# Ranks of a top-2 expert routing: doubling sums replaced by segmented scans, slots computed earlier on VectorE

## The reference, cut to what matters

```python
scores = sigmoid(x @ router_w)                    # 4096 x 16
_, top_idx = top_k(scores + expert_bias, 2)       # ties: the lower index wins
gates = sum(one_hot(top_idx) * top_scores)
shared_out = (silu(x @ w1) * (x @ w2)) @ w3       # all tokens
for e in range(16):                               # routed
    acc += (silu(xf @ w1[e]) * (xf @ w2[e])) @ w3[e] * gates[:, e]
out = x + tanh(g_ffn) * (shared_out + acc)
```

## Time and profile before

| | us |
|---|---|
| median of the runs (3) | 642.24 |
| lowest, highest | 637.35, 643.82 |
| span of the profiled execution | 568.1 |
| median less that span | 74.1 |
| PE busy in the span | 538.4 (95%) |
| DVE busy | 399.6 (70%) |
| ACT busy | 307.6 (54%) |
| POOL busy | 270.1 (48%) |

### The profile page before, as it was taken

One profiled execution on the slowest core, in us unless ns is written; L12 is line 12 of the kernel. 1 busy time (PEld: TensorE's weight loads), 2 busy tenths in 40 slices (PEclk: granted clock), 3 DMA queues, 4 the chain that ended last, 5 costly groups with the idle time before them and its releaser, 6 DMA issues.

```text
span 568.1 us, 13109 instructions
## 1 busy us (share of the span) xinstructions
PE 538.4 (95%) x4164; PEld 348.7 (61%) x4164; DVE 399.6 (70%) x890; ACT 307.6 (54%) x594; POOL 270.1 (48%) x257
## 2 busy tenths in 40 slices
PE   4899799999989999994999999999999999999997
PEld 2467676756556656653566666666666655665664
DVE  1432888867797867772788888888888736677675
ACT  2324666785226665651677777777777733333332
POOL 3001475453417787876443444334443035666770
PEclk9659999999999999997999999999999999999999
DMA  8999626338504120011233333333334123374442
GB/s 223 313 351 310 224 104 222 115 110 284 180 1 152 55 74 20 2 37 35 81 103 105 112 104 109 103 100 113 110 105 107 57 56 104 93 250 121 140 135 88
DMA packets 53228, 72.55 MB, mean 128 GB/s; under 512 B 8032, under 2 KB 43424, under 8 KB 53168
## 3 DMA queue, kind: packets, MB, share of 16 engines
q1 hardware_dynamic: 43984, 51.75, 27.9%
q0 software_dynamic: 8608, 17.91, 11.7%
q10 hardware_dynamic: 576, 2.10, 1.1%
HBM read 49.64 MB, written 22.09 MB: 126 GB/s over the span
## 4 chain that ended last, share of the span: by engine, by line
PE 68%; POOL 14%; DVE 6%; issue 5%; DMA 4%; SPq 1%; ACT 1%; DVEq 0%; POOLq 0%; ACTq 0%
PE bank L1568 17%; PE bank L1472 17%; POOL slot_token L550 12%; PE bank L1493 8%; PE bank L1594 8%; PE bank L1578 4%; PE bank L1308 3%; PE bank L1552 3%; DMA WR<-in_ctx_t 2%; PE bank L1335 2%; PE bank L1297 1%; POOL X L518 1%; DVE STAGE L917 1%; DMA xrow<-STAGE 1%; PE bank L1382 1%
## 5 line engine op out<-in xcount | busy, mean ns | idle before, releaser
L1472 PE MATMUL bank<-XTC,WS 128*128 128x512 f16 x768 | 176.1, 379 | 0.5 <-DVE ROWS L1213 0.5
L1472 PEld LDWEIGHTS bank<-XTC,WS 128*128 128x128 f16 x768 | 74.8, 98 | 78.9 <-issue 1.0
L567 POOL DMA_INDIRECT ROWS<-xrow,idx x72 | 76.8, 1067 | 97.0 <-PE bank L1552 83.7
L1568 PE MATMUL bank<-WR,XTB 128*64 x432 | 100.4, 382 | 0.7 <-DVE STAGE L1219 0.7
L1568 PE MATMUL bank<-STAGE,XTB 128*64 128x512 f16 x432 | 100.4, 382 | 0.0
L584 POOL DMA_INDIRECT ROWS<-yrow,posi x64 | 63.8, 997 | 55.0 <-DMA yrow<-ROWS 26.8
L550 POOL DMA_INDIRECT slot_token<-tokid,sloti x64 | 72.2, 1129 | 34.9 <-issue 19.2
L798 ACT ACTIVATE STAGE<-WR 128x1024 f16 x72 | 76.7, 1066 | 18.2 <-PE bank L1594 17.9
L720 ACT ACTIVATE SIL<-bank 128x512 f32<-128x512 f32 x63 | 37.6, 597 | 81.1 <-PE bank L1472 79.9
L1568 PEld LDWEIGHTS bank<-WR,XTB 128*64 128x64 f16 x432 | 44.7, 110 | 44.1 <-issue 7.7
L1112 DVE SCALAR_TENSOR_TENSOR G<-bank,SIL 128x512 f32<-128x512 f32 x63 | 43.4, 690 | 29.7 <-ACT SIL L720 29.0
(11 more groups left out here) (171 smaller groups left out, 874.5 us busy)
## 6 DMA issues: line engine op xcount, KB each, us to landing
WR<-in_routed_w SPq DMA_DIRECT2D x39, 256.0 KB, 5.3
yrow<-ROWS SPq DMA_DIRECT2D x72, 128.0 KB, 1.7
X<-in_x SPq DMA_DIRECT2D x4, 1024.0 KB, 13.0
xrow<-STAGE SPq DMA_DIRECT2D x8, 512.0 KB, 2.9
xtd<-STAGE SPq DMA_DIRECT2D x8, 512.0 KB, 2.6
out<-X SPq DMA_DIRECT2D x7, 512.0 KB, 3.3
WR<-in_ctx_t SPq DMA_DIRECT2D x4, 768.0 KB, 10.8
WR<-in_shared_w SPq DMA_DIRECT2D x3, 1024.0 KB, 14.4
```

The source lines that it names most:

```text
L567: pool.indirect_dma_start(out=XG[:, u, :], out_offset=None, in_=xrow, in_offset=bass.IndirectOffsetOnAxis(ap=idx[:, b:b + 1].bitcast(U32), ...
L1472: last = pe.matmul(acc[:, :], WS[:, wx, at:at + P], XTC[:, u, xx, k, :], start=(k == 0 and m == 0), stop=(k == KD - 1 and m == 2))
L1568: last = pe.matmul(bank[u][part, :], XTB[:, b % 4, xx, k, part], w[s], start=(k == 0 and m == 0), stop=(k == KD - 1 and m == 2), tile_posi ...
```

## The change

- `choose_lowest` now runs one segmented scan (`tensor_tensor_scan`, state = state * NEXT + EQ, where `NEXT_E` is 0 at the first expert of a tile and 1 elsewhere) and one `scalar_tensor_tensor` in place of a multiplication, a reduction and a comparison. `rev` and its iota are gone.
- `OHS`, the rank tables and the totals lie expert by tile (`[E, NT]`) where they lay tile by expert; `OHS` is written, and `PA` read, through a transposed view.
- `take_totals` and the five `sum_tiles` become one scan that reads bank 7. `before` is now minus the other triangle with the diagonal, so that the subtraction of the totals (L1052) goes. `sum_experts` has 5 instructions where it had 10, a scan of 16 elements among them, and counts rows, not blocks.
- The order on DVE: `sum_experts` and `slots_of_all` come ahead of `gate_hidden(8)`; both `slots_of_choice` and `table_slots` ahead of `gate_hidden(9)`; then `add_shared(0)` and `block_experts`. `gates` comes ahead of `gate_hidden(12)`.
- POOL takes the low half of step 9 also (POOL_TO from J + 1 to J + 2, J = 8), ahead of its scatters.
- `prepare` fills two tables of 512 elements and clears their first columns, where it cleared two of 256 and two of 8.

```diff
-        POOL_FROM, POOL_TO = 2, J + 1
+        POOL_FROM, POOL_TO = 2, J + 2
...
-            pool.memset(before[:, :], 1.0).then_inc(c_mem, 1)
+            pool.memset(before[:, :], -1.0).then_inc(c_mem, 1)
...
-                link(dve.tensor_tensor(RE, EQ, over_tiles(rev[:, :]), ALU.mult))
-                link(dve.tensor_reduce(rm[:, :], RE, AX.X, ALU.max))
-                link(dve.tensor_tensor(OH[k], over_experts(rm[:, :]), over_tiles(rev[:, :]), ALU.is_equal))
+                link(dve.tensor_tensor_scan(out=rows_flat(RE), data0=rows_flat(NEXT_E), data1=rows_flat(EQ),
+                                            initial=0.0, op0=ALU.mult, op1=ALU.add))
+                link(dve.scalar_tensor_tensor(out=OH[k], in0=RE, scalar=1.0, in1=EQ,
+                                              op0=ALU.is_equal, op1=ALU.mult))
...
-            def take_totals():
+            def sum_tiles():
+
                 dve.wait_ge(rank, 2)
-                link(dve.tensor_copy(rows_flat(INCA[:, PADT:PADT + NT, :]), bank[7][:, :]))
...
+                link(dve.tensor_tensor_scan(out=rows_flat(INC), data0=rows_flat(NEXT_T), data1=bank[7][:, :],
+                                            initial=0.0, op0=ALU.mult, op1=ALU.add))
+
+            def sum_experts():
+
+                link(dve.tensor_scalar(ni[:, :], INC[:, :, NT - 1], float(PR - 1), None, ALU.add))
                 link(dve.tensor_scalar(bi[:, :], ni[:, :], PR.bit_length() - 1, None, ALU.arith_shift_right))
...
+                link(dve.tensor_scalar(bf[:, :], bi[:, :], float(PR), None, ALU.mult))
+                link(dve.tensor_tensor_scan(out=ea[:, :], data0=ones[:, 0:E], data1=bf[:, :],
+                                            initial=0.0, op0=ALU.mult, op1=ALU.add))
+                link(dve.tensor_tensor(base_row[:, :], ea[:, :], bf[:, :], ALU.subtract))
+
+            def slots_of_all():
+
+                link(dve.tensor_tensor(PB, INC, base_row[:, :].unsqueeze(2).to_broadcast([P, E, NT]), ALU.add))
                 link(dve.tensor_tensor(rows_flat(PA), rows_flat(PB), bank[6][:, :], ALU.add))
 
             def slots_of_choice(k):
-                link(dve.tensor_tensor(EQ, OH[k], PA, ALU.mult))
+                link(dve.tensor_tensor(EQ, OH[k], PA.rearrange("p e t -> p t e"), ALU.mult))
...
-            dve.tensor_tensor(OHS, OH[0], OH[1], ALU.add).then_inc(ohs_ready, 1)
+            dve.tensor_tensor(OHS.rearrange("p e t -> p t e"), OH[0], OH[1], ALU.add).then_inc(ohs_ready, 1)
             gate_hidden(7, 1, pool=4)
-            take_totals()
-            sum_tiles(INCA, INCB, 1)
-            sum_tiles(INCB, INCA, 2)
-            sum_tiles(INCA, INCB, 4)
+            sum_tiles()
+            sum_experts()
+            slots_of_all()
             gate_hidden(8, 0, pool=5)
-            sum_tiles(INCB, INCA, 8)
-            sum_tiles(INCA, INCB, 16)
-            ends = sum_experts(INCB)
-            gate_hidden(9, 1, pool=6)
-            hidden_lo(9, 1)
-            add_shared(0)
-            gate_hidden(10, 0, pool=7)
-            slots_of_all(INCB)
-            hidden_lo(10, 0)
-            block_experts(ends)
-            gate_hidden(11, 1)
             slots_of_choice(0)
-            hidden_lo(11, 1)
             slots_of_choice(1)
             table_slots()
+            gate_hidden(9, 1, pool=6)
+            add_shared(0)
+            block_experts()
+            gate_hidden(10, 0, pool=7)
+            hidden_lo(10, 0)
+            gate_hidden(11, 1, pool=8)
+            hidden_lo(11, 1)
+            gates()
             gate_hidden(12, 0)
-            gates()
             hidden_lo(12, 0)
```

More of the change, by code:

```diff
@@ L181, in flamingo_block @@
         OH1 = arena([NT, E])
-        OHS = arena([NT, E])
-        INCA = arena([NT // 2 + NT, E])
-        INCB = arena([NT // 2 + NT, E])
-        PA = arena([NT, E])
-        PB = arena([NT, E])
+        OHS = arena([E, NT])
+        INC = arena([E, NT])
+        PA = arena([E, NT])
+        PB = arena([E, NT])
+        NEXT_E = arena([NT, E])
+        NEXT_T = arena([E, NT])
         UNDER = -(-arena_at[0] // SLOT)
@@ L207, in flamingo_block @@
         bf = sb("bf", [P, E], F32)
[L208 to L209 removed]
+        ea = sb("ea", [P, E], F32)
         base_row = sb("base_row", [P, E], F32)
@@ L491, in _ @@
             pool.affine_select(out=before[:, :], in_=before[:, :], compare_op=ALU.is_ge, fill=0.0,
-                               base=-1, pattern=[[1, P]], channel_multiplier=-1).then_inc(c_ready, 1)
-            pool.iota(row_iota[:, :], pattern=[[1, PARTS]], base=0, channel_multiplier=PARTS,
+                               base=0, pattern=[[-1, P]], channel_multiplier=1).then_inc(c_ready, 1)
+            pool.iota(row_iota[:, :], pattern=[[PR, PARTS]], base=0, channel_multiplier=PARTS * PR,
                       allow_small_or_imprecise_dtypes=True)
@@ L500, in _ @@
                                    base=2 - k, pattern=[[-4, NW]], channel_multiplier=1).then_inc(c_mem, 1)
-            pool.iota(rev[:, :], pattern=[[-1, E]], base=E, channel_multiplier=0,
-                      allow_small_or_imprecise_dtypes=True).then_inc(c_ready, 1)
             pool.memset(SDROW, 0.0).then_inc(sdrow_zero, 1)
@@ L1021, in gates @@
                     link(dve.tensor_scalar(gate[:, k, :], gsum[:, :], tgs[:, :], None, ALU.mult))
-            def take_totals():
+            def sum_tiles():
                 dve.wait_ge(rank, 2)
-                link(dve.tensor_copy(rows_flat(INCA[:, PADT:PADT + NT, :]), bank[7][:, :]))
-            def sum_tiles(src, dst, step):
-                link(dve.tensor_tensor(dst[:, PADT:PADT + NT, :], src[:, PADT:PADT + NT, :],
-                                       src[:, PADT - step:PADT - step + NT, :], ALU.add))
@@ L1032, in sum_experts @@
-            def sum_experts(inc):
-                link(dve.tensor_scalar(ni[:, :], inc[:, PADT + NT - 1, :], float(PR - 1), None, ALU.add))
-                link(dve.tensor_scalar(bi[:, :], ni[:, :], PR.bit_length() - 1, None, ALU.arith_shift_right))
-                dve.tensor_copy(bf[:, :], bi[:, :])
-                link(dve.tensor_copy(ea[:, PADE:PADE + E], bi[:, :]))
-                es, ed = ea, eb
-                step = 1
-                while step < E:
-                    link(dve.tensor_tensor(ed[:, PADE:PADE + E], es[:, PADE:PADE + E],
-                                           es[:, PADE - step:PADE - step + E], ALU.add))
-                    es, ed = ed, es
-                    step *= 2
-                ends = es[:, PADE:PADE + E]
-                link(dve.tensor_tensor(nf[:, :], ends, bf[:, :], ALU.subtract))
-                link(dve.tensor_scalar(base_row[:, :], nf[:, :], float(PR), None, ALU.mult))
-                return ends
@@ L1067, in table_slots, with block_experts @@
                                          in1=highi[:, :, :], op0=ALU.mult, op1=ALU.add).then_inc(slots_ok, 1)
-            def block_experts(ends):
+            def block_experts():
                 for s in range(PARTS):
-                    last = dve.tensor_scalar(ended[:, s, :], ends, row_iota[:, s:s + 1], None, ALU.is_le)
+                    last = dve.tensor_scalar(ended[:, s, :], ea[:, :], row_iota[:, s:s + 1], None, ALU.is_le)
                 link(last)
```

19 lines of the change are left out of this document (4 added, 15 removed).

## The result

| | us |
|---|---|
| median of the kernel after (4 runs) | 656.51 (655.24 to 658.9) |
| median of the kernel before beside it (4 runs) | 643.03 (637.35 to 650.64) |
| ratio after / before | 1.0215, 95% interval 1.0161 to 1.0269 |
| profiled execution of after: own time, span | 658.9, 656.8 |

What follows compares the result with a forecast made beforehand. PE was taken as the bound, with one wait for rows behind POOL's scatters. Gains of 7.95 (wait), 0.8 (`add_shared(0)`) and 2.4 (clock), 11.15 us, took 642.24 to 631.1 us; 8-in-10 range 627 to 637.5.

Steps and rivals of the forecast that it cites:

- The step that failed: Whole kernel: terms counted from the profile's 568.1 us span, the 74.1 us up to the 642.24 median left unchanged.
- the 7.95 us: PE's wait at the first `block_transpose` for fetched rows: gone entirely, rows ready 1.6 us ahead of PE.
- I take nothing: Seven scatter issues moved from 248-258 to 158-168 us: worth between -2 and +4.6 us, counted as nothing.
- Rival 3: DVE's scans run as a slow recurrence: whole gain eaten from 5.7 us a scan, 649 at 8 us; chance 0.03.
- The dense instruction of `choose_lowest`: DVE's choices: one dense instruction of 0.68 us beside the scan, making each choice 0.7 us shorter.
- From bank 7 to `sloti`'s end: DVE's stretch from reading bank 7 to the finished slots: 12.9 us earlier, at 155.3 against 168.23.
- `add_shared(0)`: DVE's step ahead of PE's `late_rows(8)`: runs earlier, gaining 0.8 of PE's 1.63 us wait.
- Scatters: POOL's 64 scatters: first starts at about 158.2, 10.3 us earlier; count and pitch of 1.43 us stay.
- Rival 1: At the first block POOL's chain still ends last; with a start at 163, 634.3 to 636.7 us; chance 0.11.
- The clock behind it: PE from first transpose to `block_hidden(1)`: full clock, 3.6 us in place of 5.98, 2.4 gained.
- Rival 4: Whole kernel: only the removed DVE work is gained, PE being 95% busy; 642 or within 1%; chance 0.04.
- rival 2: PE's steps 10 to 13 each wait 1 to 2 us; price 3 to 5 us, at worst 636 to 638; chance 0.06.

Runs made afterwards that it cites:

- e5: The kernel after, unchanged, on another chip, starved: 652.86 us (649.75 to 654.88 in 6 runs); no ratio given.
- e6: The kernel before with the new order on DVE (not quite after's) and POOL_TO = J + 2, but its old sums and choices: 643.28 us.
- e11: The kernel after with POOL's first scatter held back to about before's start, starved: 647.44 us, ratio 1.0103 to before.
- e13: The kernel after with 16 one-column matmuls added ahead of the text stage, shifting PE's instructions, starved: 652.02 us, ratio 1.017 to before.
- e7_after: The kernel after, unchanged, on a chip that didn't starve it: 559.71 us, ratio 0.9824 to before's 569.72.
- e14: The kernel after with each tile's pair of scatters waiting until the pair before has landed, starved: 622.69 us, ratio 0.9713 to before.
- e12: The kernel after without its 64 scatters, every block fetching token 0, starved: 575.01 us, ratio 0.8969 to before.
- e2: The kernel after with the first scatter held back to about before's start, unstarved: 570.39 us, ratio 1.0019 to before.
- e8: The kernel after with the first scatter held back to before's start, unstarved, in a later set: 570.31 us, ratio 1.0004 to before.

## Why the prediction was wrong

**The step that failed** is "I count from its span, 568.1 us, and leave the 74.1 us between it and the median, 642.24, as they are". They aren't time around the span. 2.1 us are (658.9 - 656.8; 1.7 for before). The some 72 us left were a second condition of the same kernel: its run of 643.21 has a span of 641.5 and a mean clock of 0.926, its run of 569.72 has 568.0 and 0.970. All terms were priced in the unstarved execution and promised for the starved one, where they don't hold: in none of the five starved profiles with scatters at full pace (the first one of after, e5, e6, e11, e13) does PE wait for fetched rows, so the 7.95 us, the largest term, weren't there to be gained. (Before itself left no starved trace.) The sum named the gap and drew nothing from it; no rival asked what 74 us outside a kernel could be, and none had scatters that stop PE. What made it slower, as far as is shown, was the term put at nothing, "I take nothing" for the scatters moved forward: where PE is starved, putting them back made the new kernel 4.6 us faster (e13 against e11, below).

**In the condition of the profile the mechanism was right.** e7_after gains 10.0 us by the medians; 11.15 were forecast. Its profile is to be read by differences: it reaches bank 7 at 142.98, 3.45 us ahead of before's 146.43, by code that the change leaves nearly alone. The granted clock of its first 60 us was 0.86 against 0.80, and the four profiles of after reach bank 7 anywhere between 142.98 and 146.71, starved or not. So 13.9 us between the two spans are 3.45 of this and 10.5 of the change. Term by term, from the timelines of e7_after, first DVE's:

```profile
131.26 1.47 DVE L1003 SCALAR_TENSOR_TENSOR WR<-WR 128x512 f32<-128x512 f32 x1
132.76 0.69 DVE L1007 SCALAR_TENSOR_TENSOR WR<-WR 128x512 f32<-128x512 f32 x1
...
142.98 1.22 DVE L1019 TENSOR_TENSOR_SCAN WR<-WR,bank 128x512 f32<-128x512 f32 x1 [1.56 <-PE bank L1422]
...
147.56 1.04 DVE L1037 TENSOR_TENSOR WR<-WR 128x512 f32<-128x512 f32 x1
...
152.05 0.22 DVE L1045 SCALAR_TENSOR_TENSOR sloti<-lowi,highi 128x64 int32<-128x64 int32 x1
...
152.80 1.65 DVE L1067 SCALAR_TENSOR_TENSOR X<-bank,tgs,X 128x256 f32<-128x256 f32 x4
```

- *Scan*: 1.22 us, 1.09 taken. Rival 3, the dear scan, falls. Half throughput as the Trainium skill has it ("DVE: opcode table, instruction layouts, handler registers and perf-mode slots", "Datapath and trigger behaviour") would be 1.2, an estimate; the trace agrees.
- *Transposed view*: 1.04, 1.07 taken; the write of `OHS` took 1.05. The 1.35, an estimate worked out from the Trainium skill's "Vector Engine (DVE) Microarchitecture Reference", "Measured stream behaviour on trn2", isn't borne out at this step of 32 words; the page's 2.5 ns are for a destination, or both sources, in steps of 24 words, and it has no row for one source in such small steps.
- *The dense instruction of `choose_lowest`* is 1.47 and not 0.68, twice L1007 of the same size. A choice is thus no shorter than before. `OHS` ends at 140.90, 0.06 us ahead of PE's first matmul that reads it (140.96; before 144.05 and 144.51). The slack was just used up, so that the wrong price cost next to nothing is luck.
- *From bank 7 to `sloti`'s end*: 152.27 - 142.98 = 9.3 us against 21.8 before, 12.5 earlier; 12.9 forecast.
- *`add_shared(0)`*: PE waits 1.26 for it, not 1.63: 0.4 gained, 0.8 forecast.

PE's and POOL's timelines, and the window behind the first block's start:

```profile
154.59 0.38 PE L1466 MATMUL bank<-WS,wv 128*128 128x256 f16 x2 [1.26 <-DVE X L1067]
...
252.38 2.78 PE L1466 MATMUL bank<-WS,GS 128*128 128x256 f16 x24
...
255.00 0.38 PE L1525 MATMUL bank<-ident,ROWS 128*128 128x128 f32 x2
...
258.97 0.40 PE L1541 MATMUL bank<-WR,XTB 128*64 x1
```
```profile
154.95 1.16 POOL L546 DMA_INDIRECT slot_token<-tokid,sloti  x1 [0.18 <-issue]
...
243.38 1.28 POOL L546 DMA_INDIRECT slot_token<-tokid,sloti  x1 [0.30 <-issue]
...
248.88 1.21 POOL L563 DMA_INDIRECT ROWS<-xrow,idx  x1 [1.89 <-DMA idx<-slot_token]
```
```profile
253.00:258.00 5.00, 4.44 (x40) 3.62 (x40) 3.10 (x6) 1.57 (x4) 2.80 (x4) 1.00 0.30 82
```

- *Scatters*: the first starts 154.95 - 142.98 = 11.97 us behind bank 7, 10.1 less than before; 10.3 forecast. One takes (243.38 - 154.95) / 63 = 1.40 us, 1.43 taken.
- *The wait for the rows*: 7.95 us, gone as forecast. Rows take 266.93 - 264.04 = 2.9 us from the fetch's issue, so they were there at about 251.8, 3.2 us ahead of PE; 1.6 forecast. Rival 1 falls.
- *The clock behind it*: it stays at 1.00. From the transpose to `block_hidden(1)` 3.97 us, not 5.98: 2.0 gained, 2.4 forecast.

7.95 + 0.4 + 2.0 = 10.3 us, measured 10.0. Rival 4 falls with the ratio 0.9824, and rival 2 with PE's waits, none of them in steps 10 to 13.

**Where after's time went in the starved condition.** The spans of the starved and the unstarved profile of the same kernel, 656.8 and 554.2, split at three places of PE's stream of matmuls and weight loads (counted in the trace: instruction 1908, where the slow stretch begins, 2996, about the first `block_transpose`, and 8000):

| | starved | unstarved | difference |
|---|---|---|---|
| to 1908 | 172.3 | 168.3 | 4.0 |
| 1908 to 2996 | 165.0 | 87.0 | **77.9** |
| 2996 to 8000 | 184.6 | 181.1 | 3.5 |
| 8000 to the end | 134.9 | 117.7 | **17.1** |

Of the first 4.0 us, 3.7 are there when bank 7 is read (146.71 against 142.98), ahead of any scatter: they are the clock at the start again, not starvation. The second difference is the stretch of the scatters. The fourth is the last part, in which POOL gathers the routed rows (L580); DVE has there, among others, this wait for nothing shown (its waits from 520 us on):

```profile
DVE G L1091 <- issue: 16.8, 6, 5.0
```

No such wait is in e7_after's last part. What stands behind it is the same as in the slow stretch: `silu` starts up to 7.0 us behind PE's matmuls. It does so by 5.5 to 7.8 us in every starved profile, with and without scatters and also in e14, and by less than 0.1 in every unstarved one. PE's signals come late in both places where POOL issues indirect DMAs in close succession, the 64 scatters and the 64 gathers; that the gathers are the cause in the second place was not tested.

**Why the change is slower there.** An earlier start of the scatters is worth 10 us where PE waits for their result. Starved, PE doesn't, and the start costs instead. In one starved set the early start (e13, the shifted kernel, which stands for after) took 652.02 us (650.72 and 653.32), the late start 647.44 (645.9 to 649.46) and before 643.55. So of the 8.5 us by which the early start is slower than before, putting the start back returns 4.6. That is shown, if by few runs. The 10 us of the unstarved gain are missing as well, for want of a wait to shorten. The other 3.9 us, seen as e11's ratio of 1.0103, have no cause shown: before's starved execution left its span and clock and no trace, and its runs in that set, 639 to 654, lie around all four of the late start.

Why an earlier start should cost anything is only partly shown. What is measured: with the start at 156.5 to 158.7 us PE slows 13.5 to 13.7 us later in three profiles, with the start at 165 to 168 it does so 21 to 24 us later, while the end moves with the scatters. With the early start they at first follow one another every 1.27 us. From 169 us on, in e7_after, DVE makes the low halves of the routed weights (L1106), and single scatters beside them take longer, here on DVE and on POOL:

```profile
169.24 1.85 DVE L1106 SCALAR_TENSOR_TENSOR WR<-WR 128x768 f16<-128x768 f32 x2
```
```profile
169.23 0.97 POOL L546 DMA_INDIRECT slot_token<-tokid,sloti  x1 [0.30 <-issue]
170.51 1.43 POOL L546 DMA_INDIRECT slot_token<-tokid,sloti  x1 [0.30 <-issue]
```

An early start has over ten scatters in a nearly unbroken row ahead of these. The late start has none, and e6, which slows 24 us behind its first scatter, eight, two of them longer (1.24 and 1.36 us). That a dense row brings the stop sooner would fit; once PE is stopped DVE is idle too, and the pace stays at (240.09 - 158.69) / 63 = 1.29. It was argued, not tested, and density alone isn't enough, as e7_after has the same row and isn't starved. e14 shows that with pauses, at 2.2 us a scatter, nothing stops; whether the lower pace or the waits for landing do it isn't told apart.

**Open.** What puts the kernel into the starved condition is outside of it and wasn't found: the kernel before is in it too, in all four runs beside the first result, and one chip was seen in both. What it is in hardware that keeps PE from issuing is open as well; e13 excludes a fixed place in the instruction stream, e12 anything but the scatters for the first stretch. Two more things can be read from the starved profile of after. Slow transfers of instructions aren't it: the one fetch of 16 KB in the stretch, at 212.4, takes 0.98 us, as such fetches do in before (0.99 to 1.29). And from 180 us on PE's matmuls start by multiples of about 0.7 us apart (1.4, 2.1, 2.8, 3.5, 4.2), whichever matmul it is; what sets that step nothing here says. e14 beats both kernels in the starved condition (622.69 against 643.55 and about 652). It wasn't run out of it; there the slower pace would cost roughly the 43 us that it waits for the rows, an estimate. Of the two kernels compared here, after is the better one unstarved (560 against 570 us) and before when starved (643 against 656).

## What to carry to other kernels

Before any sum is made, hold the profiled execution's span against the timed median: a gap far beyond the 2 us that lie outside a span meant here that the profile showed another condition than the one that was timed, and no term of it held for the other. A long run of small indirect DMAs from POOL isn't free because POOL has time: its worst price may be paid by PE, and starting it earlier can make that dearer (4.6 us here). An edit whose whole worth is one transfer's start is best tried alone, by holding that start back in the new kernel, as e2, e8 and e11 do. And when an engine is idle, compare the end of what it waits for with its own start: here that showed signals of PE's that came up to 65 us late.

## What the runs showed that wasn't expected

- While POOL issues 64 indirect scatters at 1.27 to 1.29 us each, PE can be held to one matmul in 1.4 to 2.8 us for 83 us (172.3 to 255), with 4 instructions on DVE where there were 72; with waits for landing between pairs, 4.33 us a pair, in the same condition not at all.
- In that stretch ACT starts up to 65.6 us behind the end of the matmuls that it waits for, and up to 7.8 us behind it in the last part of every starved profile; unstarved it is under 0.1 us in the last part.
- The slow stretch begins 13.5 to 24 us behind the first scatter, not with it, and the scatters' own packets don't pile up in it (through within 1.0 us in 63 of 64).
- `scalar_tensor_tensor` with `is_equal` and `mult` on 512 float32 took 1.47 us, with `mult` and `add` 0.69.
- A scan over 512 float32 took 1.22 us, from PSUM as from SBUF.
